# Layer-1 attention of a two-layer transformer block on one core: the row of negated maxima reaches q by a VectorE transpose and a 4 KB transfer instead of TensorE matmuls and a ScalarE copy

## What is computed

```python
xn = layer_norm(x, ln_gamma, ln_beta)
q, k, v = heads(xn @ Wq), heads(xn @ Wk), heads(xn @ Wv)      # 16 heads of 64
att = jnp.einsum('bhid,bhjd->bhij', q, k) / DIM_HEAD ** 0.5
att = att + alibi_bias(S, N_HEADS)[None]                      # -slope * |i - j|
p = jax.nn.softmax(att, axis=-1)
out = jnp.einsum('bhij,bhjd->bhid', p, v)
return out.transpose(0, 2, 1, 3).reshape(B, S, INNER) @ Wo
```

## Time and profile before

| | |
|---|---|
| median of 3 runs | 2350.16 us (2349.41 to 2352.84) |
| span of the profiled execution | 2369.8 us |
| the profiled execution's own time outside the span | none is given; the span stands 19.6 us above the median |
| instructions | 40846 |
| TensorE busy | 2244.5 us (95%) |
| mean granted TensorE clock | 0.978 |
| mean DMA rate | 39 GB/s |

### The profile page before, as it was taken

One profiled execution on the slowest core, in us unless ns is written; L12 is line 12 of the kernel. 1 busy time (PEld: TensorE's weight loads), 2 busy tenths in 40 slices (PEclk: granted clock), 3 DMA queues, 4 the chain that ended last, 5 costly groups with the idle time before them and its releaser, 6 DMA issues.

```text
span 2369.8 us, 40846 instructions
## 1 busy us (share of the span) xinstructions
PE 2244.5 (95%) x11022; PEld 1400.4 (59%) x11023; DVE 1779.8 (75%) x4554; ACT 1299.5 (55%) x1725; POOL 1384.8 (58%) x751
## 2 busy tenths in 40 slices
PE   4999999899999999999999999999999999789995
PEld 2556566455656565656556565656565564439884
DVE  4687886787778878787788777887878777665555
ACT  0233323466666666666666666666666663344442
POOL 2112111387767777777778676777777776543331
PEclk7999999999999999999999999999999999899997
DMA  7013202000000100000100000010000000311114
GB/s 259 1 64 128 83 1 92 27 16 18 16 13 12 38 13 15 12 17 15 34 13 14 18 13 15 12 38 13 16 12 14 18 8 11 137 42 48 47 44 133
DMA packets 86502, 91.25 MB, mean 39 GB/s; under 512 B 19060, under 2 KB 71284, under 8 KB 86264
## 3 DMA queue, kind: packets, MB, share of 16 engines
q1 hardware_dynamic: 82072, 81.35, 10.9%
q0 software_dynamic: 4352, 8.99, 1.1%
HBM read 57.63 MB, written 36.33 MB: 40 GB/s over the span
## 4 chain that ended last, share of the span: by engine, by line
PE 83%; DVE 6%; issue 3%; POOL 3%; ACT 1%; DMA 1%; SPq 1%; another core or an unknown queue 0%; POOLq 0%; DVEq 0%; ACTq 0%
PE P L1980 19%; PE P L1944 11%; PE P L1965 10%; PE P L1966 9%; PE P L2090 3%; PE P L2394 3%; PE P L1987 3%; PE P L2076 2%; PE P L1893 2%; PE P L1998 2%; PE P L1949 1%; PE P L2364 1%; PE P L2365 1%; PE P L2366 1%; PE P L2384 1%
## 5 line engine op out<-in xcount | busy, mean ns | idle before, releaser
L1588 ACT ACTIVATE big<-P 128x1024 f32<-128x1024 f32 x512 | 512.5, 1021 | 192.4 <-PE P L1966 81.9
L1014 DVE CUSTOM_DVE_ANT_0 big<-P,near 128x512 f32<-128x512 f32 x512 | 348.7, 681 | 215.3 <-PE P L1944 213.1
L1980 PE MATMUL P<-big,V 128*64 128x512 f32 x2048 | 482.4, 602 | 1.0 <-ACT big L1594 1.0
L628 POOL TENSOR_TENSOR spair<-spair,big 128x1024 f32<-128x1024 f32 x192 | 457.7, 2384 | 16.7 <-DVE hp L788 1.3
L628 POOL TENSOR_TENSOR opair<-opair,big 128x1024 f32<-128x1024 f32 x192 | 457.6, 2384 | 15.0
L1944 PE MATMUL P<-kq 96*128 96x512 f32 x1008 | 415.0, 432 | 3.1 <-DVE kq L1002 1.4
L1965 PE MATMUL P<-kq 97*128 97x512 f32 x1024 | 408.1, 399 | 1.2 <-ACT big L1588 1.1
L1966 PE MATMUL P<-kq 128*128 128x512 f32 x1024 | 405.7, 396 | 0.0
L1017 DVE TENSOR_REDUCE mhalf<-P 128x1 f32<-128x512 f32 x512 | 349.2, 682 | 74.3 <-PE P L1944 63.6
L1944 PEld LDWEIGHTS P<-kq 96*128 96x128 f32 x1008 | 181.3, 189 | 203.8 <-issue 101.9
L615 POOL TENSOR_TENSOR big<-big,sinv 128x512 f32<-128x512 f32 x64 | 82.0, 1281 | 336.4 <-DVE sinv L988 336.3
(11 more groups left out here) (320 smaller groups left out, 3752.0 us busy)
## 6 DMA issues: line engine op xcount, KB each, us to landing
slots<-later SPq DMA_DIRECT2D x4, 4224.0 KB, 15.1
kq<-auxrows SPq DMA_DIRECT2D x64, 128.0 KB, 2.3
big<-in_wex SPq DMA_DIRECT2D x8, 768.0 KB
xt<-slots SPq DMA_DIRECT2D x76, 66.0 KB, 1.8
near<-in_aux SPq DMA_DIRECT2D x64, 64.0 KB, 1.8
big<-yrows SPq DMA_DIRECT2D x8, 512.0 KB, 7.2
wqk_hi<-wparts SPq DMA_DIRECT2D x62, 64.0 KB, 1.8
wqk_lo<-wparts SPq DMA_DIRECT2D x62, 64.0 KB, 1.8
```

Source lines behind the costliest of these rows:

```text
L628: pool.tensor_tensor(psum8[s][:, :], psum8[s][:, :], pfull[:, j % RING, :], ALU.add).then_inc(S["p_added"], 1)
L1014: dve.tensor_tensor_reduce(waste, P[:, bank, :], near[s][:, left:left + HALF], -1.0, 3.0e38, ALU.add, ALU.min, mhalf[:, i, t:t + 1]).then_ ...
L1588: act.activation(pfull[:, j, :], banks(2 * (j % 2)), ACT.Exp, scale=DH1 ** -0.5).then_inc(S["exp_done"], 1)
L1980: mm = pe.matmul(P[64 * i:64 * i + 64, 4, :], V1[:, j, s, :], half(pfull[:, j, :], i), start=(j == 0), stop=(j == T - 1))
```

## The change

`turn_max` and `maxima` are gone. `max_both` writes the minima of each 32 partitions separately, so that `mneg` is [32, 32] with column 4t + b for block t and quarter b; the new `max_rows` waits for them and transposes 32x32 on VectorE into `mrows` [32 rows, 32]; row 4t + b then holds the 32 queries of that quarter in order. SyncE's new `load_max` waits for this and copies the 4 KB to row 96 of `Qa`, 32 pieces of 128 bytes, with `m_in` counting 16 for each transfer. `max_half` of a head's first block now waits for the reductions of the head before, not for `m_in`. The dummy matmuls in the hand-over are 8 and 13 in place of 5 and 10.

```diff
--- before.py
+++ after.py
@@ -66,6 +66,7 @@
 FAR = float(1 << 20)
 XBUF, YBUF = 4, 4
 
+M_IN = 16
 ST_AT, EXP_AT, PV_AT, COPIED_AT, NORM_AT = 1, 1, RING, 1, 3
 ADD_AT, SUM_AT, WO_AT, X_AT = T - 1, 2, 1, 2
 HEADS = B * H1
@@ -291,7 +292,8 @@
         spair = sb("spair", [128, N])
         kvs = opair[:, 0:D + H0]
         mhalf = sb("mhalf", [128, NHALF, T])
-        mneg = sb("mneg", [128, T], F32R)
+        mneg = sb("mneg", [32, 4 * T], F32R)
+        mrows = sb("mrows", [4 * T, 32])
 
         P = ctx.enter_context(nc.psum_tensor("P", [128, 8, HALF], F32))
 
@@ -446,6 +448,13 @@
                 block = a["aux"][g, NAUX:NAUX + NDIAG, :].rearrange("r (q c) -> (r q) c", c=128)
                 sp.dma_start(near[s][:, ZERO:ZERO + 128], block).then_inc(S[f"tab_in{s}"], 16)
 
+            def load_max(n, s):
+
+                sp.wait_ge(S["m_row"], n + 1)
+                sp.sem_inc(G["passed"], 1)
+                row = Qa[s][MROW:MROW + 1, :].bitcast(F32).rearrange("o (i c) -> o i c", c=32)
+                sp.dma_start(row, mrows[:, :]).then_inc(S["m_in"], 16)
+
             tail = blank[:, B * quarter * chunk:].rearrange("p (a c) -> p a c", a=4)
             sp.dma_start(tail, over(empty[:, 0:rest // 4], [128, 4, rest // 4])).then_inc(G["filled"], 16)
 
@@ -469,6 +478,7 @@
                     sp.wait_ge(S["hT_in"], 32)
                     sp.sem_inc(S["h_ok"], 4)
                     sp.wait_ge(G["wparts_out"], 32)
+                    load_max(0, 0)
                     sp.wait_ge(S["qk_mm"], 4)
                     load_qk(2, 0)
                     load_qk(3, 1)
@@ -506,12 +516,14 @@
                 sp.wait_ge(S["biased"], da)
                 sp.sem_inc(G["passed"], 1)
                 load_near(g, 0)
+                load_max(at(2 * p + 1), 1)
                 sp.wait_ge(S["st_mm"], ub)
                 sp.sem_inc(G["passed"], 1)
                 load_aux(g + 1, 1)
                 sp.wait_ge(S["biased"], db)
                 sp.sem_inc(G["passed"], 1)
                 load_near(g + 1, 1)
+                load_max(at(2 * p + 2), 0)
 
             next_pair(0, 2, qk=False)
             with sp.Fori(1, PAIRS - 1) as q:
@@ -523,6 +535,7 @@
                 next_pair(b * PAIRS + PAIRS - 1, 0, b)
             with sp.Fori(0, PAIRS - 1) as q:
                 next_pair((B - 1) * PAIRS + q, 2 * q + 2)
+            load_max(HEADS - 1, 1)
             for s in range(2):
                 sp.wait_ge(S[f"wh_in{s}"], 32 * ALL_PAIRS - 16)
                 sp.wait_ge(S["wv_in"], 32 * ALL_PAIRS)
@@ -1018,7 +1031,18 @@
 
             def max_both(n):
                 dve.wait_ge(S["max_red"], (n + 1) * T * NHALF)
-                dve.tensor_tensor(mneg[:, :], mhalf[:, 0, :], mhalf[:, 1, :], ALU.min).then_inc(S["max_both"], 1)
+                for b in range(4):
+                    rows = slice(32 * b, 32 * b + 32)
+                    dve.tensor_tensor(mneg[:, b::4], mhalf[rows, 0, :], mhalf[rows, 1, :], ALU.min).then_inc(S["max_both"], 1)
+
+            def max_rows(n):
+
+                dve.wait_ge(S["max_both"], 4 * n + 4)
+                if not isinstance(n, int):
+                    dve.sem_inc(G["passed"], 1)
+                if not isinstance(n, int) or n > 0:
+                    dve.wait_ge(S["m_in"], M_IN * n)
+                dve.transpose(mrows[:, :], mneg[:, :].bitcast(F32)).then_inc(S["m_row"], 1)
 
             def bias(s, n, j):
 
@@ -1067,6 +1091,7 @@
                 maxima((7, 0), (7, 1))
                 if ahead:
                     max_both(n + 1)
+                    max_rows(n + 1)
                 if behind:
                     invert(o, n - 1, 2)
                 if ahead == 2:
@@ -1178,6 +1203,7 @@
             for k in range(CH0 * NHALF - 6, T * NHALF):
                 early_max(k)
             max_both(0)
+            max_rows(0)
             c_residual(B - 1)
             q_low(1, 1, 0)
             k_low(1, 1, 0)
@@ -1211,6 +1237,7 @@
                     k_low(0, 2, 1)
                     q_low(0, 2, 1)
             max_both(1)
+            max_rows(1)
 
             head(0, 1, behind=1)
             with dve.Fori(1, ALL_PAIRS - 1) as p:
@@ -1573,10 +1600,6 @@
                 act.wait_ge(S["o_norm"], 2 * n - 2 + NORM_AT)
                 act.activation(sinv[s][:, :], P[:, bank, :], ACT.Copy).then_inc(S["s_copied"], 1)
 
-            def maxima(s, n):
-                act.wait_ge(S["m_row"], n + 1)
-                act.activation(Qa[s][MROW:MROW + 1, :], banks(6, 2, slice(0, 1)), ACT.Copy).then_inc(S["m_in"], 1)
-
             def exps(n, j):
 
                 k = T * n + j
@@ -1627,8 +1650,6 @@
                 if ahead == 2:
                     q_high(s, n + 2, 1)
                     k_high(s, n + 2, 1)
-                if ahead:
-                    maxima(o, n + 1)
                 if ahead == 2:
                     q_again(s, n + 2)
                 if behind:
@@ -1681,7 +1702,6 @@
                             k_again(0, 0)
             q_high(1, 1, 0)
             k_high(1, 1, 0)
-            maxima(0, 0)
             exps(0, 0)
             exps(0, 1)
             q_high(1, 1, 1)
@@ -1701,7 +1721,6 @@
             k_high(0, 2, 0)
             q_high(0, 2, 1)
             k_high(0, 2, 1)
-            maxima(1, 1)
             q_again(0, 2)
 
             head(0, 1, behind=1)
@@ -1936,24 +1955,16 @@
                     pe.wait_ge(S[f"aux_in{s}"], 8 * (n - s) + 16)
                     pe.wait_ge(S["q_lo"], 2 * n + 2)
                     pe.wait_ge(S["k_lo"], 2 * n + 2)
-                    if not isinstance(n, int) or n > 0:
-                        pe.wait_ge(S["m_in"], n)
-                if t > 0:
+                if not isinstance(n, int) or n > 0 or t > 0:
 
                     pe.wait_ge(S["max_red"], (n * T + t) * NHALF + i - 1)
                 pe.matmul(P[:, 6 + i, :], tile(Qa[s][0:MROW, :], t), half(Ka[s][0:MROW, :], i), start=True, stop=True).then_inc(S["max_mm"], 1)
 
-            def turn_max(n):
-                pe.wait_ge(S["max_both"], n + 1)
-                for t in range(T):
-                    mm = pe.matmul(P[0:1, 6 + t // TPH, (t % TPH) * 128:(t % TPH + 1) * 128], mneg[:, t:t + 1], identr[:, :], start=True, stop=True)
-                mm.then_inc(S["m_row"], 1)
-
             def scores(s, n, j):
 
                 k = T * n + j
                 if j == 0:
-                    pe.wait_ge(S["m_in"], n + 1)
+                    pe.wait_ge(S["m_in"], M_IN * (n + 1))
                     pe.wait_ge(S["q_dup"], n + 1)
                     pe.wait_ge(S["k_dup"], n + 1)
                 if not isinstance(k, int) or k > 0:
@@ -2061,8 +2072,6 @@
                 weigh(s, n, p, 3)
                 weigh(s, n, p, 4)
                 weigh(s, n, p, 5)
-                if ahead:
-                    turn_max(n + 1)
                 weigh(s, n, p, 6)
                 weigh(s, n, p, 7)
 
@@ -2190,8 +2199,7 @@
             early_qk(1, 0, 5)
             for k in range(EARLY, T * NHALF):
                 early_max(k)
-            turn_max(0)
-            keep_busy(4, 5)
+            keep_busy(4, 8)
             pe.wait_ge(S["xb_done"], EACH["xb_done"] * B)
             scores(0, 0, 0)
             keep_busy(4, 1)
@@ -2230,9 +2238,7 @@
                     max_half(1, 1, t, i)
                 if t == 4:
                     project_qk(0, 2, 1)
-            keep_busy(2, 5)
-            turn_max(1)
-            keep_busy(2, 5)
+            keep_busy(2, 13)
             pe.wait_ge(E["c_kept"], NHALF * B)
 
             head(0, 1, behind=1)
```

## The result

| kernel | median us | lowest to highest | executions | span of the profiled execution | its own time |
|---|---|---|---|---|---|
| before, beside the changed kernel | 2351.5 | 2349.41 to 2354.99 | 4 | 2369.8 (shown above) | |
| changed | 2326.81 | 2322.4 to 2330.95 | 4 | 2320.6 | 2322.4 |

The ratio is 0.9895, with a 95% interval of 0.9876 to 0.9914: faster by about 1%, 24.7 us of medians, where the forecast had 32.6. The new time lies inside the range given, 2311 to 2333, and 9 us above the forecast of 2317.6.

The account below looks back on a forecast made before the run. TensorE's queue was taken as the bound in layer-1 attention. -35.3 + 1.2 + 0.3 + 1.2 = -32.6 us, from a median of 2350.16, gave 2317.6 us, range 2311 to 2333.

Parts of the forecast that it names:

- TensorE bounds the stage, and what leaves its queue leaves the time: Layer-1 attention: TensorE busy all 24.00 us of a stretch, so removed matmuls shorten the time unless a new wait arises.
- 62 turns at 0.57 us of chain are 35.3 us: Loop and its two peeled ends: removing each head's eight turn matmuls saves their queue time, 35.3 us in all.
- (a): First hand-over, head 0: nothing hides the row, so scores start 1.0 to 1.5 us later; 1.2 taken.
- (b): Second hand-over, head 1: dummies and another wait follow the minimum; loss between nothing and 1.2 us, 0.3 taken.
- (c): Three changes of batch: GpSimd's addition holds VectorE's minimum, q's low part comes late; 0.5 to 0.6, then 0.3 each, 1.2 us.
- Rival 2: VectorE's longer work, or GpSimd's hold in every head, delays q's low part; gain partly or wholly eaten, 2350; chance 0.07.
- a delay dies out: Loop of held minimum, late scaling and late additions: takes 22.3 us, less than a head's 23.56, so lateness doesn't persist.
- VectorE's tail: Four minima without overlap, a wait and a transpose per head: next instruction 0.74 us later, with margins left in ordinary heads.
- rival 1: The row's transfer in 32 small pieces comes late and scores wait; about 2379 us at 4.4 us landing; chance 0.07.
- The 512 KB load behind it, costed at nothing: SyncE's queue at a change of batch: GpSimd's load behind the row costs nothing, up to 0.5 us in the bad bound.
- Rival 3: First exponential of each head: its 0.3 us margin is gone and scores wait; half of 35.3 lost, 2335; chance 0.06.
- ScalarE's copy costed at nothing: Each head: removing ScalarE's copy of 1.01 us gains nothing, since ScalarE waits for work behind it.

Follow-up runs that it names:

- e3: Changed kernel with eight unused matmuls of the old turn's shape put back inside the weighing run, where the turn stood: 2362.32 us, ordinary period 24.14.
- e7: Changed kernel with eight unused turn matmuls behind the last weighing matmul, before the next head's first maxima: 2367.85 us, ordinary period 23.84.
- e4: Changed kernel with the row first copied to a spare tile, SyncE waiting for that before sending it to q: 2355.06 us, ordinary period 23.72.
- e10: Changed kernel with its four minima as one-input reductions and every second head's row transfer issued behind the next pair's h_lo load: 2308.1 us, ratio 0.9801.
- e5: Changed kernel with one one-input 128x8 reduction, a transpose by blocks and four 1 KB transfers instead of one of 4 KB: 2342.16 us, ratio 0.9882.
- e1: The changed kernel, unaltered, timed again beside the kernel before: 2329.33 us, ratio 0.9901.

## Why the prediction was right, and where it was off

- **TensorE bounds the stage, and what leaves its queue leaves the time.** Right. The step "62 turns at 0.57 us of chain are 35.3 us" was too small: it took the turn's own row and left out what the turn did to the row behind it. It could have been read in the chain before, where twelve weighing matmuls took 2.73 and eight 1.87, more than two thirds of it (1.82). e3 gives 0.72, e7 0.42. The forecast period of 23.56 was 23.42.
- **"What is given back", (a).** At the first hand-over the scores start 2.92 us behind the start of the minima, where the earlier trace rows have 2.00: 0.9 later, forecast 1.2. Right.
- **(b) and (c).** This is the step that failed. "I take 0.3" and "1.2 in all" stood for the second hand-over and the changes of batch; together with (a) they were 2.7 us, and 20 were given back. The mechanism was named, in (c) and in the rule of the Trainium skill beside it, "GPSIMD Engine Reference", section "1. Specifications", that two SBUF inputs on VectorE contend with GpSimd: the runs agree, 2273 ns against 165 with one input. Its size was wrong in three ways. I let the hold stay what it was before, 1.47 us, and added the tail; but the third of the minima was caught at the start of an addition and held for 2.27, so that the four take 3.12. I priced TensorE's wait at 0.5 to 0.6 at the first change and 0.3 at the others; it was 2.1, 1.8 and 1.8. And I left out the clock that can fall behind such a wait: the first change, where it fell, lost 3.9 us, the others, where it stayed up, 2.6. In (b) the four minima took 2.80 us, and the second head's first scores waited 2.49 us for the row, where I had 0.3.
- **The other three places.** Four heads behind each change of batch GpSimd has one more operation of 2.4 us, which makes its additions end behind the minima once more (here 888.3, where one minimum took 1.62 us); the 25.3 among the first four periods is the same. The prediction has no term for it. Periods of 24.9 to 25.2 are some 4 us in all.
- **Rival 2, the hold in every head.** Right to give it little: its argument that a delay dies out fits, as 57 of 64 heads have no such wait. In ordinary heads GpSimd ends at 1005.95 and the minima start at 1006.72: 0.8 us apart, forecast 1.1. The rival's price was not for every head, but for seven of them.
- **VectorE's tail.** Four minima that don't overlap, as forecast. The addition up to the reciprocal is 1.02 us (reciprocal 1.11 behind the first minimum, 0.09 before) and not 0.74: the wait for the last minimum's end puts 0.23 us of idle time in front of the transpose, and I had only 0.03. It didn't decide: VectorE still idles 0.35 us before the next maxima, forecast 0.7.
- **The transfer (rival 1).** Landing 1.7 us after issue, forecast 1.8 to 2.3; a slack of 1.5, forecast 1.2 to 1.7; and e4 confirms it with 1.47. Right. Only SyncE's issue, 0.53 us where the loads of 64 KB take 0.34, was longer than thought. The 512 KB load behind it, costed at nothing, was worth the 1.2 us that e10 took back.
- **Rival 3.** Nothing of the gain is lost at the exponential: ordinary periods have the whole 0.72.
- **ScalarE's copy costed at nothing.** e3 has ScalarE without the copy and TensorE with the turn, and its period is that of the kernel before. Right.

The sum with measured terms: 63 periods x 0.718 = 45.2, less 7, 9 and 4, is 25.2; the heads show 25.1 and the medians 24.7.

That the time came to lie in the range is partly luck. Two terms were too small, and they work against each other: the gain by some 10 us and the loss by some 17. With the turn at its forecast 35.3 us and the 20 us given back as measured, the time would have been near 2335, above the range.

**Open.** Why the clock fell behind some waits of 1.4 to 2.1 us and not behind others of 1.3 to 1.9 isn't shown: in two executions of the changed kernel it fell in different places. Of the 20 us it has about 3 (1.3 at the first change, some 1.5 in the fourth period, by the same periods where it stayed up). And why one chip runs the kernel before some 17 us slower than two others, outside the heads, stays open.

## What to carry to other kernels

Price a removed instruction by the chain with and without it, its neighbours included: eight matmuls of 0.57 us were worth 0.72 inside a run of another kind and 0.42 at its end. Before one instruction with two inputs in on-chip memory is made into several, look at each place where GpSimd's work runs late, the rare ones (a new batch, an extra operation once in a batch) above all, and write them with one input where a reduction over a pair says the same: that edit was worth 19.7 us here, nearly as much as the change itself gave. And a transfer that is hidden can still cost something, by what stands behind its issues in the queue: in e5 a 512 KB load 3 us late cost 3.7 us at each change of batch, and the order alone brought it back.

## What the runs showed of the hardware

- A VectorE instruction with two inputs in on-chip memory can be held to the end of a GpSimd addition of 2.38 us: 0.16 us became 2.27. As a reduction with one input the longest of 256 was 0.165 us.
- After 2.12 us of TensorE idle time, and in e5 after 1.93, the granted clock fell to 0.50, and matmuls of 0.23 us took 0.43. After 1.84 us it stayed at 1.00, twice; after 1.85 in e1 it fell. Where it fell behind such a wait, a head lost some 1.3 to 1.5 us more.
- A transfer of 4 KB in 32 pieces into one partition lands 1.7 us after issue, but its issue holds SyncE's queue for 0.53 us; four of 1 KB hold it for 2.7.
- In the chain, the first matmuls of another kind behind weighing matmuls take some 0.15 us more (two maxima matmuls 0.66 there, 0.51 behind the turn).
